# A two-layer graph network on one NeuronCore: X U21 formed a step early, P and K in one product, fp16 transposes in the first layer, and a tile's later work spread over the next tile

## The reference

```python
# first layer: quantised graph convolution
h = relu(layernorm(x));  support = relu(quant(h) @ quant(weight));  x = x + adj @ quant(support) * scales
# second layer, on h = relu(layernorm(x)); R = (adj + I) / row sums
Xf = Xa = h
for s in range(2):
    logits = (Xa @ W1) @ W2 @ (Xa @ W3).T          # 2048 x 2048
    A  = softmax over the fewest top entries of a row that hold 0.9 of its softmax
    Xf = R @ Xf;   Xa = A @ Xa
    Z += Xf @ U1[s] + Xa @ U2[s]
out = x + layernorm(h + Z) * gamma + beta
```

## Time and profile before

| | us |
|---|---|
| median of three runs (lowest, highest) | 1463.36 (1462.64, 1469.3) |
| the profiled execution | 1465.6 |
| its span | 1463.8 |

### The profile page before, as it was taken

The page is one execution under the profiler, slowest core; times in us unless marked ns, Lnnn a source line. Parts: engine busy times, 40 slices in busy tenths (PEclk is TensorE's granted clock), DMA queues, the critical chain, the costliest instruction groups (busy, mean ns, idle before and its releaser), DMA issues.

```text
span 1463.8 us, 18743 instructions
## 1 busy us (share of the span) xinstructions
PE 1239.3 (85%) x6458; PEld 607.9 (42%) x6458; DVE 1113.8 (76%) x1880; ACT 600.1 (41%) x1129; POOL 291.1 (20%) x233
## 2 busy tenths in 40 slices
PE   0348999997699689999989899789799999999994
PEld 0123555553244245444545454234344444444442
DVE  6985777773699999269949900499899989879667
ACT  1332444444831244455454343760234364353331
POOL 3312343432122213011122111011101011011011
PEclk9888999999899899999999999989999999999998
DMA  6124455442134211121110140524421121120244
GB/s 209 57 86 169 178 190 188 179 161 90 44 118 143 86 49 66 42 75 51 37 65 30 32 157 30 194 72 146 127 66 58 37 94 43 38 72 30 97 153 175
DMA packets 57687, 143.95 MB, mean 98 GB/s; under 512 B 9664, under 2 KB 9664, under 8 KB 53248
## 3 DMA queue, kind: packets, MB, share of 16 engines
q1 hardware_dynamic: 57600, 142.91, 28.3%
HBM read 90.72 MB, written 52.17 MB: 98 GB/s over the span
## 4 chain that ended last, share of the span: by engine, by line
PE 63%; issue 15%; ACT 9%; DVE 6%; POOL 4%; DMA 4%; POOLq 0%; SPq 0%; DVEq 0%; ACTq 0%
PE AB L785 15%; PE UB L647 9%; PE AB L788 8%; PE RB L745 6%; PE AB L637 4%; PE AB L630 3%; PE TB L656 3%; PE XB L647 3%; PE RB L647 3%; PE RB L747 2%; ACT squares L972 2%; POOL RT L541 2%; PE LB L720 2%; DMA AD<-z_d 2%; DMA AD<-xu_d 1%
## 5 line engine op out<-in xcount | busy, mean ns | idle before, releaser
L1268 DVE SCALAR_TENSOR_TENSOR WS<-E,g 128x2048 bf16<-128x2048 f32 x128 | 313.7, 2501 | 4.9 <-ACT E L992 3.8
L785 PE MATMUL AB<-XR,turns 128*128 128x512 f16 x1024 | 242.1, 380 | 0.0
L745 PE MATMUL RB<-VR,turns 128*128 128x512 f16 x704 | 165.7, 388 | 23.2 <-DMA turns<-adj_parts 23.2
L1355 DVE TENSOR_REDUCE g<-E 128x1 f32<-128x2048 f32 x32 | 73.0, 2280 | 126.5 <-ACT E L965 126.5
L785 PEld LDWEIGHTS AB<-XR,turns 128*128 128x128 f16 x1024 | 100.0, 98 | 105.4 <-issue 0.7
L541 POOL TENSOR_TENSOR RT<-RT,AD 128x512 f32<-128x512 f32 x32 | 57.5, 1795 | 382.6 <-ACT RT L1004 382.6
L788 PE MATMUL AB<-XR,turns 128*128 128x512 f16 x512 | 131.5, 380 | 0.0
L1029 ACT ACTIVATE turns<-TB 128x512 f16<-128x512 f32 x128 | 75.3, 594 | 124.9 <-PE TB L662 124.8
L745 PEld LDWEIGHTS RB<-VR,turns 128*128 128x128 f16 x704 | 68.7, 100 | 105.8 <-DMA turns<-adj_parts 27.1
L647 PE MATMUL UB<-UW,XT 128*128 128x512 f16 x384 | 88.2, 380 | 27.4 <-ACT XT L917 27.2
L965 ACT ACTIVATE E<-LB 128x512 f32<-128x512 f32 x128 | 75.4, 596 | 40.1 <-PE LB L721 38.0
(11 more groups left out here) (266 smaller groups left out, 2032.2 us busy)
## 6 DMA issues: line engine op xcount, KB each, us to landing
turns<-adj_parts SPq DMA_DIRECT2D x64, 512.0 KB, 3.8
E<-adjT SPq DMA_DIRECT2D x16, 1024.0 KB, 5.1
adj_parts<-turns SPq DMA_DIRECT2D x16, 1024.0 KB, 3.9
z_d<-UO SPq DMA_DIRECT2D x31, 256.0 KB, 2.0
XR<-x SPq DMA_DIRECT2D x4, 1024.0 KB, 12.0
WS<-U SPq DMA_DIRECT2D x4, 1024.0 KB, 5.3
x_d<-E SPq DMA_DIRECT2D x16, 256.0 KB, 2.6
xu_d<-UO SPq DMA_DIRECT2D x16, 256.0 KB, 2.0
```

The source lines that it names most:

```text
L745: i = mm(bank[:, :], AT[:, 0, j, :], VR[:, j, k % 2, :], start=(k == 0), stop=False)
L785: mm(AB[:, :], ET[:, 0, j, :], XR[:, j, y_, :], start=(j == 0 and y_ == 0), stop=False)
L1268: return v.scalar_tensor_tensor(junk[t % 2], e, g4[:, k, t:t + 1], e, op, ALU.mult, accum_out=g4[:, F_, t:t + 1])
```

## The change: what it does

- **X U21 in step 0.** In step 0, `w_product` forms W = Xa U21 (12 more products per tile, into XB); `w_out` on ACT copies it to `WF` and its high half to `XHL`, POOL makes the low half (`post`), and SP stores these halves in place of the features' own. Step 1 then multiplies A by W and needs no transposes and no weight products: its tile ends with one copy from the bank to `UO` (`a_out`). U21 stays in SBUF (`UV`); the trip through DRAM goes.
- **P and K formed once.** `WPK` holds W1 W2 beside W3, so 12 products of 128 columns give P on partitions 0 to 63 and K on 64 to 127; ACT writes the second copies (five copies where there were three). In step 0 this product uses UB.
- **fp16 transposes in the first layer.** `x_halves_turned` transposes the two halves out of `XR` (8 fp16 transposes), after a quarter of the low-half products, and waits for `s_xh` and `s_xl`, the high half (ACT) and the low half (POOL). One ACT copy of 1024 columns takes both out. `x_turned` before the low-half products and `x_rest` go there, and DVE's wait for `s_xT`.
- **Later work spread.** In step 0, the transposes, X U20, X U21, P and K of tile t - 1 stand between the chunks of tile t; a group's last tile is finished in the next `group_start`, inside an R tile. The products A X and R V use AB and RB in turn.
- **R tiles.** The high half of R's tile has two buffers (`AT`, `AH`). R tiles 9 to 15 are run whole, 1, 2, 2 and 2 of them at the start of groups 0 to 3. `terms(g + 1)` on ACT comes after the first two chunks of group g are taken out.

```diff
+R_FIRST = 9
+R_BEHIND = (1, 2, 2, 2)
...
             logits(s, 1)
-            r_tiles(s, 1, R_EARLY)
-            terms(s, 1)
-            r_tiles(s, R_EARLY, R_FIRST)
+            r_tiles(s, 1, R_FIRST)
             for g in range(NG):
-                if 0 < g < NG - 1:
-                    terms(s, g + 1)
-                if g < R_BEHIND:
-                    r_behind(s, R_FIRST + g * (1 + G // 2))
+                group_start(s, g)
                 pairs(s, g)
...
+            def x_halves_turned(n):
+                pe.wait_ge(s_pkc, n + OPEN)
+                pe.wait_ge(s_xh, n + 1)
+                pe.wait_ge(s_xl, n + 1 + OPEN)
+                for h in range(2):
+                    for k in range(KC):
+                        c = h * KC + k
+                        i = tr(XB[:, :].bitcast(F16)[:, c * P:(c + 1) * P],
+                               XR[:, bass.ds(n, 1), h, k * P:(k + 1) * P].rearrange("p o d -> p (o d)"), ident[:, :])
+                i.then_inc(s_xT, 1)
...
             def adj_product_lo(t, h, n=None):
...
-                    if j == T // 2 and n is not None:
-                        x_rest(n)
+                    if j == T // 4 and n is not None:
+                        x_halves_turned(n)
...
-                for w in range(2):
-                    i = three(XB[:, w * P:(w + 1) * P], lambda k: WPK[:, k, w, 0, :], lambda k: WPK[:, k, w, 1, :], xh, xl)
-                i.then_inc(s_pk, 1)
+                three(bank[:, 0:P], lambda k: WPK[:, k, 0, :], lambda k: WPK[:, k, 1, :], xh, xl).then_inc(s_pk, 1)
...
+            def w_product(t):
+                three(XB[:, :], xh, xl, lambda k: UV[:, k, 0, :], lambda k: UV[:, k, 1, :]).then_inc(s_w, 1)
...
# PE, a tile of the second layer (post: step 0, from the group's second tile on)
+                bank_free(s, first_use(g) + c)
+                terms_product(qq, 0, bank)
+                e_rest(qq, 2)
+                e_turned(qq, slot, 3)
+                if post:
+                    x_turned(t - 1 + T)
                 if ahead:
                     logits_chunk(s, s * NG + g + 2, t + 2 * G, 0)
                     logits_chunk(s, s * NG + g + 2, t + 2 * G, 1)
+                terms_product(qq, 1, bank)
+                e_rest(qq, 3)
+                if more:
                     e_turned(qq + 1, after, 0)
+                if post:
+                    x_rest(t - 1 + T)
+                terms_product(qq, 2, bank)
+                if post:
+                    u_product(t - 1)
...
+                if post:
+                    w_product(t - 1)
...
+                terms_product(qq, 3, bank)
...
+                if post:
+                    p_and_k(t - 1)
...
# PE, the start of a group
+                e_turned(t + s * T, t % (2 * G), 0)
+                e_turned(t + s * T, t % (2 * G), 1)
+                if g < NG - 1:
+                    r_whole(s, g, count - 1)
...
# ACT, the end of a tile's A X product
+            def a_out(s, g, t, slot, bank):
+                act.wait_ge(s_a, NC * (t + s * T + 1) + OPEN)
+                act.wait_ge(s_rden, s * NG + g + 1)
+                if s == 0:
...
+                    a(XF[:, :], bank[:, :], ACT.Copy, scale=rden[:, slot:slot + 1]).then_inc(s_xf, 1)
+                else:
...
+                    a(UO[:, :], bank[:, :], ACT.Copy, scale=rden[:, slot:slot + 1]).then_inc(s_ue, 1)
...
# ACT, the start of a group
+                e_hi(t + s * T, 0)
+                e_hi(t + s * T, 1)
+                if g < NG - 1:
+                    terms(s, g + 1)
+                    r_out(s, first_r(g) + count - 1, bank_of(g, count - 1))
```

More of the change, by code:

```diff
@@ L44, with first_use, first_r @@
 OPEN = 1
[L45 to L48, removed]
 RUN = 4
+R_FIRST = 9
+R_BEHIND = (1, 2, 2, 2)
 R_HI = 2 * T
 R_ALL = R_HI + T
-R_CUTS = (0, 4, 17, 24, 28, 41, R_ALL)
+def first_use(g):
+    return R_FIRST + sum(R_BEHIND[:g]) + g * G
+def first_r(g):
+    return R_FIRST + sum(R_BEHIND[:g])
+BANK_USES = [("r", t) for t in range(R_FIRST)]
+for _g in range(NG):
+    BANK_USES += [("r", first_r(_g) + j) for j in range(R_BEHIND[_g])] + [("a", G * _g + i) for i in range(G)]
 class Chain:
@@ L219, in weights_src, with step_order @@
             return u.rearrange("(k p) d -> p k d", p=P)
[L223 removed]
+        def step_order(s, logits, terms, r_tile, r_tiles, group_start, pairs, last_post):
             logits(s, 0)
@@ L385, in fin_out, with stores, group_start @@
                 sp.dma_start(out[slice(*FIN[b])].rearrange("t p d -> p t d"), y).then_inc(s_out, 16)
-            def tile(s, t, h, r, more):
-                if s == 0:
-                    x_store(t + T, t)
-                if h == 1 and r is not None:
-                    if more:
-                        at_lo_in(s, r + 1)
-                        ad_in(s, r + 1)
-                    r_store(s, r)
-                if s == 0:
-                    z0_store(t)
-                else:
-                    z_in(t)
-                    if t < T - 1:
-                        y_store(t)
-                if h == 0 and r is not None and more:
-                    at_hi_in(s, r + 1)
+            def stores(t):
+                x_store(t)
+                z0_store(t)
+            def group_start(s, g):
+                if s == 0 and g:
+                    stores(G * g - 1)
+                for j in range(R_BEHIND[g]):
+                    r = first_r(g) + j
+                    r_done(s, r, r % 2)
             def pairs(s, g):
@@ L418, in pairs @@
                 for i in range(G):
-                    r = r_of(g, i // 2)
-                    tile(s, g * G + i, i % 2, r, r is not None and r + 1 < T)
+                    t = g * G + i
+                    if s == 0:
+                        if i:
+                            stores(t - 1)
+                    else:
+                        z_in(t)
+                        if t < T - 1:
+                            y_store(t)
                     if last and i == 1:
@@ L730, in logits, with r_products @@
                         logits_chunk(s, s * NG + g, t, c)
-            def r_products(s, t, a, b, bank=RB, ahead=False):
-                if t is None:
-                    return
+            def r_products(s, t, odd, bank, a, b):
                 r = t + s * T
@@ L794, in tile @@
                 qq = t + s * T
[L795 removed]
                 slot, after = t % (2 * G), (t + 1) % (2 * G)
[L797 to L804 removed]
+                post, more, ahead = s == 0 and i > 0, i + 1 < G, g + 2 < NG
+                c = R_BEHIND[g] + i
+                bank = bank_of(g, c)
+                if i == 0:
                     e_rest(qq, 0)
@@ L881, in _ @@
+            step_order(0, logits, nothing, r_tile, r_tiles, group_start, pairs, last_post)
+            step_order(1, logits, nothing, r_tile, r_tiles, group_start, pairs, last_post)
         @block.scalar
```

458 lines of the change are left out of this document (223 added, 235 removed).

## The result

The changed kernel takes 1482.47 us (median of 4 runs, 1481.2 to 1483.2) against 1464.7 (median of 4 runs, 1462.64 to 1469.3) for the kernel before on the same chip: ratio 1.0121, 95% interval 1.0099 to 1.0144. It is 1.2% slower; 1440 was forecast. The profiled execution has a span of 1480.6 us against 1463.8, so +16.8, and this is what the two traces have to explain.

A forecast was written before the change was run, and what follows sets the result against it. The limits were taken as a DVE-PE loop in the first layer, PE's list in step 0's groups and DVE in step 1. Span 1463.8 + 25 - 1 - 19 - 16 - 12.5 = 1440.3; forecast 1440 us, range 1414 to 1463.

The forecast's parts named there:

- First layer, +25: First layer: PE waits 1.3 us for POOL's low half, then transposes; +1.67 us per tile over 15 tiles, +25 us.
- rival (e): First layer: waiting brings the lower clock for 12 products, 2.6 us per tile, total 1479 us; chance 0.05.
- Step 0 up to the first group, -25: Before step 0's first group: the 12.56 us PE hole goes and first A X products start earlier, 25 us gained.
- Step 0's groups: Step 0's groups: 20.0 us tiles and 1.6 us waits at three group starts; +6 us to the last P and K.
- Step 1 and the end, -28.5: Step 1: two DVE gaps shrink to 21.7 us, -16; the end after the last `rden`, -12.5 us.
- rival (c): Step 1: time follows PE's work there too, 85 us gained instead of 28.5, total 1384 us; chance 0.07.
- Rival (d): Step 0's tiles: ACT's order of copies loses 3 us per tile, 48 us, total 1488 us; chance 0.10.

The follow-up runs named there:

- e11: e2 with the first layer's eight fp16 transposes after 12 instead of 4 low-half products; 1449.68 us, ratio 0.9902 to the kernel before.
- e5: Changed kernel with step 0's group starts reordered: low halves of two turned chunks formed before ACT's exponentials, no wait for POOL's sum ahead of them; 1457.17 us.
- e6: Changed kernel with W formed from its four high products instead of all twelve; 1457.38 us.
- e12: Changed kernel with all R tiles reading the adjacency's high half from one buffer again; 1492.52 us, ratio 1.0174 to the kernel before.
- e1: Changed kernel with the first layer's four fp32 transposes and one-product rest put back as before; 1441.49 us, ratio 0.9847 to the kernel before.
- e4: Changed kernel with X's halves formed early and the eight fp16 transposes put ahead of the first low-half product; 1437.13 us, ratio 0.9822 to the kernel before.
- e2: Changed kernel with one POOL line moved: X's low half formed before the low halves of P and K; 1459.52 us, ratio 0.9968 to the kernel before.
- e9: Changed kernel with the edits of e4 and e5, and DVE's two first-layer passes exchanged; 1395.2 us, ratio 0.9512 to the kernel before.

## Why the prediction was wrong

The ledger by the prediction's own steps:

- **First layer, +25: the failed step.** The mechanism was named rightly (POOL's low half late behind DVE's pass, PE waiting ahead of the transposes) and its wait of 1.3 us was 1.42. The term was mis-sized in three places. The transposes were taken at the lower of two bounds, 0.064, "since type and width are those of the narrow product"; they took 0.118, just above the upper bound of 0.11, and it is their place that sets this and not their type: 0.055 in e11. The low clock, rival (e) priced at 2.6 us in each tile, came in every third tile with 1.0. And the last two tiles, whose chain nothing covers, were counted like the others: from L505 of tile 14 to the logits it is 31.2 us against 22.0, 9.2 more where 2 x 1.67 = 3.3 had been given them. (e5, e6 and e12, with the same first layer, have 28.3 to 28.4 there and 272.4 to 274.4 in the whole row, so these two figures are good to about 3 us.) In tiles 1 to 14 the excess is 0.1 (wait) + 0.43 (transposes) + 0.33 (clock) = 0.9 a tile, of the measured 0.94 (2.61 less 1.67). The rule from the Trainium skill's page "TensorE: Matmul & The Clock Gate", section "Part 4: PE-mode transpose", that transposes don't count as busy, would add them to the gap. With fp32 turns (e1, 103 to 345) the clock of the layer was 0.99, and with the fp16 transposes moved (e4, 103 to 343) 0.98, against 0.94 after; no run here isolates the rule.
- **Step 0 up to the first group, -25: -20.4.** The hole before the first group is gone. Missing are 4.6 us. The wait in ACT's order at group 0 is 5.4 long, and e5, which removes it, gives 3.8 back. The short waits between R tiles were put at about 5 us, and those in the trace of before add up to 3.8.
- **Step 0's groups, the other failed step.** Tiles of 20 us came out right, and W eats what the spreading gives (e6). "At three group starts PE waits for ACT's exponentials and R copy about 1.6 each" was wrong: I had laid out ACT as exponentials, one copy out of R, low chunk. `r_out` holds two copies with POOL's sum between them, and the sum takes 3.2 us beside DVE. With it the wait is 5.3 at groups 1 and 2 (2.5 at group 3), and the products behind it run at the lower clock level (e5: 12.7 us idle, 8.6 clock). By these numbers the row is off by 2 x (5.26 - 1.6) + (2.46 + 0.29 - 1.6) + 8.6 = 17.0 us, and it was off by 16.5. Of the 22.5 us by which this stretch grew e5 gives back 21.3.
- **Step 1 and the end, -28.5: right, -25.5.** The two gaps from `rden` to the end of the first pass that were 26.3 and 33.3 before are 20.8 and 20.8 after (forecast 21.7), and PE's shorter list gave nothing further, so rival (c) falls. The end is 73.0 us after `rden` instead of 70.3. No run isolates these gaps; they are read from the traces.

The timeline of DVE in step 1, kernel after, `rden` and the next end of a first pass, answers to the earlier trace rows:

```profile
1203.08 0.17 DVE L1608 TENSOR_SCALAR rden<-g 128x4 f32<-128x4 f32 x1
1223.83 0.16 DVE L1463 TENSOR_SCALAR g<-tot 128x4 f32<-128x4 f32 x1
1305.62 0.17 DVE L1608 TENSOR_SCALAR rden<-g 128x4 f32<-128x4 f32 x1
1326.37 0.17 DVE L1463 TENSOR_SCALAR g<-tot 128x4 f32<-128x4 f32 x1
1407.56 0.17 DVE L1608 TENSOR_SCALAR rden<-g 128x4 f32<-128x4 f32 x1
```

The groups are 102.5 and 101.9 us, where about 101 was forecast. Rival (d), slower by ACT's order, had the right kind of cause and the wrong place: not inside the tiles (their copies fit) but at the group starts. That 1482 lies beside its 1488, and beside the 1479 of (e), is a coincidence: neither cause came in the size or the place that its price was worked out from. The two misses had one pattern. Both waits were seen, the second at a third of its length; in both, the forecast left what the waiting does to the work behind it at nothing.

## What to carry to other kernels

Before adding a wait, write out the whole list of the engine that releases it, down to the second copy inside a helper, with the durations that its instructions have beside the other engines and not alone. Price a wait on TensorE as its length plus what the next instructions lose: here 21.3 us came back for 12.7 us of waiting. An operation that must wait is best put in a gap that is there anyway: moving the transposes and two elementwise instructions was worth 45 us without removing any work.

## What the runs showed of the hardware

- Eight fp16 transposes of 128 columns took 0.94 us to the next product when PE had waited 0.9 us of products earlier (e2) or right ahead of them (after), and 0.44 to 0.45 behind 12 or 16 unbroken products (e11, e9). The granted clock was 1.00 in all four, and at 0.50 they took 0.96 (after, 312.34). Why an earlier wait makes them dear isn't shown.
- A POOL instruction that started while DVE's two-input pass ran ended after that pass, whichever one it was: L513 took 2.41 us against 0.42, L505 2.71 against 1.15 (e2), the sum L544 3.19 against 1.27.
- With two waits in a tile of 16.7 us, 1.14 and 1.42, part of every third tile's products ran at the lower clock level (in e5, with the same first layer, five of thirteen tiles); with 1.14 and 0.17 in one of 15.5 (e2), or 0.72 in one of 14.2 (e4), none did. The waits of 5.3 us were followed by products at half the clock each time, and so was the one of 2.46 at group 3 (eight products in 3.33 us).
